# The memory of lines in a Trainium2 kernel: weighing one tile later, the state's decay on ScalarE, the tails added in two operations

## The reference, cut to what matters

```python
write_lines = exterior(w1, w2)            # 6 numbers, scaled to length 1
read_lines = exterior(r1, r2)
Jw = write_lines @ J6
outer = Jw[..., :, None] * Jw[..., None, :]                      # 6 x 6
M_all[t] = sum over s < t of decay ** (t - s) * outer[s]   # written as a scaled cumsum
rd_M = einsum('bhti,bhtij->bhtj', read_lines, M_all)
score_M = sum(rd_M * read_lines); score_M2 = sum(rd_M * rd_M)
alpha = sigmoid(iter_mix)
mem_score = (1 - alpha) * score_M + alpha * score_M2
gated = mean over heads of sigmoid(mem_score * mem_scale) * gate
out = (seq_out + gated * mem_val) @ out_w.T + out_b
```

## Time and profile before

| | us |
|---|---|
| median of 3 runs | 1944.21 (1939.68 to 1946.05) |
| the profiled execution: its time / its span | 1945.89 / 1944.0 |
| PE busy | 1876.9 (97% of the span) |
| DVE busy | 1614.2 (83%) |
| ACT busy | 1501.3 (77%) |
| POOL busy | 916.5 (47%) |
| turns 0 to 5 of the memory of lines, first multiply of turn 0 to the reciprocal | 1149.12 to 1227.41 |
| turns 6 and 7 and the first output chunks | 1227.41 to 1252.40 |

### The profile page before, as it was taken

One profiled execution on the slowest core, in us unless ns is written; L12 is line 12 of the kernel. 1 busy time (PEld: TensorE's weight loads), 2 busy tenths in 40 slices (PEclk: granted clock), 3 DMA queues, 4 the chain that ended last, 5 costly groups with the idle time before them and its releaser, 6 DMA issues. The chain is left out here.

```text
span 1944.0 us, 61233 instructions
## 1 busy us (share of the span) xinstructions
PE 1876.9 (97%) x22590; PEld 1112.2 (57%) x22590; DVE 1614.2 (83%) x5474; ACT 1501.3 (77%) x4121; POOL 916.5 (47%) x548
## 2 busy tenths in 40 slices
PE   7999999999999999999999998899999999999998
PEld 3777763577775343444444367436777635777743
DVE  6899965899995678999999769869999658999855
ACT  5999994799997354777777754469999947999963
POOL 2788860588881040000000046338888506888800
PEclk9999999999999987999999999999999999999999
DMA  6221220122221040111111000002221201222301
GB/s 187 47 50 44 50 62 6 35 46 48 49 62 23 6 160 25 42 41 42 42 42 42 21 6 2 2 19 46 47 50 44 62 6 36 50 48 46 71 12 43
DMA packets 76138, 85.63 MB, mean 44 GB/s; under 512 B 17135, under 2 KB 50499, under 8 KB 75715
## 3 DMA queue, kind: packets, MB, share of 16 engines
q1 hardware_dynamic: 75647, 81.70, 16.8%
q10 hardware_dynamic: 196, 0.02, 0.0%
HBM read 21.16 MB, written 8.39 MB: 15 GB/s over the span
## 5 line engine op out<-in xcount | busy, mean ns | idle before, releaser
L333 ACT ACTIVATE probs<-probs,negmax 128x128 f32<-128x128 f32 x1024 | 401.8, 402 | 1.1 <-DVE negmax L408 0.6
L2170 ACT ACTIVATE gprobs<-ps_global 128x1024 f32<-128x1024 f32 (+3 forms) x384 | 291.5, 811 | 125.7 <-PE ps_global L1635 103.0
L288 POOL TENSOR_TENSOR rot<-rot 128x1024 f32<-128x1024 f32 x128 | 302.6, 2364 | 144.2 <-DVE rot L378 144.2
L294 POOL TENSOR_TENSOR qk<-rot,cnorm 128x1024 f32<-128x1024 f32 x128 | 244.0, 1906 | 170.5 <-issue 146.8
L301 POOL TENSOR_TENSOR probs<-probs,iden 128x1024 f32<-128x1024 f32 x128 | 242.9, 1898 | 45.7 <-DVE iden L416 44.9
L1865 DVE TENSOR_REDUCE maxes<-ps_global 128x1 f32<-128x512 f32 (+2 forms) x384 | 222.1, 639 | 11.4 <-PE ps_global L1598 6.5
L408 DVE CUSTOM_DVE_ANT_0 probs<-ps_attn,masks 128x128 f32<-128x128 f32 x1024 | 226.4, 286 | 0.7 <-issue 0.5
L333 ACT ACTIVATION_READ_ACCUMULATOR probs<-probs,negmax 128x1 f32 x1024 | 204.2, 199 | 0.0
L1593 PE MATMUL ps_global<-kq 48*128 48x512 bf16 (+3 forms) x768 | 197.3, 346 | 7.0 <-DVE maxes L1865 1.8
L374 DVE TENSOR_TENSOR rot<-ps_attn,rotary 128x512 f32<-128x512 f32 x256 | 175.2, 684 | 2.6 <-PE ps_attn L199 2.1
L2100 POOL CAST m_parts<-m_turn 32x128 bf16<-32x128 f32 x16 | 4.5, 281 | 364.4 <-DVE m_turn L1879 364.4
(11 more groups left out here) (220 smaller groups left out, 4531.1 us busy)
## 6 DMA issues: line engine op xcount, KB each, us to landing
v_first<-v_second SPq DMA_DIRECT2D x256, 128.0 KB, 2.3
hs<-z_a SPq DMA_DIRECT2D x256, 32.0 KB, 1.9
ln<-z_b SPq DMA_DIRECT2D x56, 128.0 KB, 2.3
kq<-split_scratch SPq DMA_DIRECT2D x64, 96.0 KB
kq<-split_scratch SPq DMA_DIRECT2D x64, 64.0 KB
split_scratch<-parts SPq DMA_DIRECT2D x8, 384.0 KB, 4.1
split_scratch<-gprobs SPq DMA_DIRECT2D x6, 384.0 KB, 4.1
x_tok<-in_x_dram SPq DMA_DIRECT2D x4, 512.0 KB, 6.4
```

The costliest lines, as they stand in the source:

```text
L288: nc.gpsimd.tensor_tensor(a, a, b, ALU.add).then_inc(C["rot_sum"], 1)
L294: nc.gpsimd.tensor_tensor(qk[:, k % 2, :].rearrange("p (h d) -> p h d", d=DH), rot_a[:, k % 2, :, :], cnorm[:, k % 2, :].unsqueeze(2).to_b ...
L333: last = nc.scalar.activation(probs[:, k % 2, slot, :], probs[:, k % 2, slot, :], ACT.Exp, scale=-1.0, bias=negmax[:, k % 2, slot:slot + 1 ...
L2170: nc.scalar.activation(probs[:, step % RING, 2 * p:2 * p + 2, 0:w], ps[:, S0 + 2 * p:S0 + 2 * p + 2, 0:w], ACT.Exp).then_inc(C["p2_exp"], 1)
```

## The change

Four edits, all in the memory of lines.

1. `weigh(t-1)` instead of `weigh(t)`: in turn t DVE makes blend, weight and score of the tile before, ahead of `sum_squares(t+2, 0)`; in the last turn `weigh(7)` is made as well. The tile `read` becomes double for this.
2. On DVE the last two multiplies (6 and 7) are put ahead of `read_memory(t, 1)`.
3. A new function `fade(t+1)` on ACT, the last of its turns 0 to 5, makes state * decay in four activations of 144 elements into the tile `faded` (a part of `ln_s`). `advance` waits for it and adds the tails from PSUM in two additions of 288 elements; `advance(0)` keeps the four old instructions.
4. ACT's `scale_lines(t)` is moved behind copies 6 and 7.

```diff
-        read, plain, blend = [behind.take(HB * LINE).rearrange("p (x c) -> p x c", x=HB) for _ in range(3)]
+        read = behind.take(2 * HB * LINE).rearrange("p (k x c) -> p k x c", k=2, x=HB)
+        plain, blend = [behind.take(HB * LINE).rearrange("p (x c) -> p x c", x=HB) for _ in range(2)]
...
             def advance(k):
                 wait(dve, "ml_tail", k + 1)
                 wait(dve, "ml_state", k)
...
                 wait(dve, f"ml_row{(k + 1) % 2}", 16 * GROUP * ((k + 1) // 2))
+                if k > 0:
+                    wait(dve, "ml_faded", k)
+                    for half in range(2):
+                        at = slice(half * GROUPS // 2, (half + 1) * GROUPS // 2)
+                        last = nc.vector.tensor_tensor(state[:, (k + 1) % 2, at, :].rearrange("p q n -> p (q n)"),
+                                                       faded[:, at, :].rearrange("p q n -> p (q n)"),
+                                                       ps[:, TAIL_BANKS[half], 0:2 * STATE_ROWS], ALU.add)
+                    last.then_inc(C["ml_state"], 1)
+                    return
...
                 all_terms(5, 6)
+                if valid(t - 1):
+                    weigh(t - 1)
                 if valid(t + 2):
                     sum_squares(t + 2, 0)
+                multiplies(6, 8)
                 if valid(t):
                     read_memory(t, 1)
-                multiplies(6, 8)
-                if valid(t):
+                if t == LAST:
                     weigh(t)
                 if valid(t + 2):
                     clip(t + 2, 0)
...
+            def fade(k):
+                wait(act, "ml_state", k)
+                for q in range(GROUPS):
+                    last = nc.scalar.activation(faded[:, q, :], state[:, k % 2, q, :], ACT.Identity, scale=A["whole"][:, q:q + 1])
+                last.then_inc(C["ml_faded"], 1)
...
-                lefts(2, 5)
-                if valid(t):
-                    scale_lines(t)
-                lefts(5, 6)
+                lefts(2, 6)
                 if valid(t + 2):
                     square_line(t + 2, 0)
                 lefts(6, 8)
+                if valid(t):
+                    scale_lines(t)
                 if valid(t + 2):
                     inverse(t + 2, 0)
                     square_line(t + 2, 1)
                     inverse(t + 2, 1)
+                if 0 < t + 1 < LAST:
+                    fade(t + 1)
```

More of the change, by code:

```diff
@@ L1441, in global_attention_pass @@
             "ml_outer", "ml_tail", "ml_state", "ml_row0", "ml_row1", "ml_m", "ml_term", "ml_read", "ml_plain", "ml_blend", "ml_weight",
-            "ml_score", "ml_turned", "ml_out"))
+            "ml_score", "ml_turned", "ml_out", "ml_faded"))
     U2 = P2_STEPS
@@ L1481, in global_attention_pass @@
         state = shared.take(2 * GROUPS * STATE_ROWS).rearrange("p (k q n) -> p k q n", k=2, q=GROUPS)
+        faded = squares[:, :, :].rearrange("p k t -> p (k t)")[:, 0:GROUPS * STATE_ROWS].rearrange("p (q n) -> p q n", q=GROUPS)
         first = Arena(early[:, :])
@@ L1912, in read_memory @@
                 wait(dve, "ml_term", USES_M * k + (3 if half == 0 else USES_M))
-                nc.vector.reduce_sum(read[:, first * B:end * B, :].rearrange("p x c -> p (x c)"),
+                nc.vector.reduce_sum(read[:, k % 2, first * B:end * B, :].rearrange("p x c -> p (x c)"),
                                      term[:, first * B * PAIRS_6:end * B * PAIRS_6].rearrange("p (x j) -> p x j", j=LINE), AX_X
@@ L1919, in weigh @@
                 wait(dve, "ml_plain", k + 1)
-                flat = read[:, :, :].rearrange("p x c -> p (x c)")
+                flat = read[:, k % 2, :, :].rearrange("p x c -> p (x c)")
                 nc.vector.scalar_tensor_tensor(out=blend[:, :, :].rearrange("p x c -> p (x c)"), in0=flat, scalar=A["alpha"][:, 0:1],
```

## The result

The changed kernel took 1961.74 us (median of 4 runs, 1957.0 to 1963.1) against 1945.13 us before (4 runs, 1939.68 to 1947.17): a ratio of 1.0082, 95% interval 1.007 to 1.0094. It is slower by 16.6 us; 10.8 were forecast, and the range ended at 1961. The profiled execution had a span of 1960.0 us against 1944.0. One later run of the kernel before, in the session of experiments 5 to 8, took 7420.19 us and is left out of every ratio.

What follows compares the result with a forecast made beforehand. DVE was taken to set the turn's period (busy 12.14 of 12.83 us). Per turn -1.67 + 0.56 + 2.15 = +1.04; six turns +6.3 plus last two turns +4.5 gave +10.8, 1955.0 us, range 1949 to 1961.

Steps and rivals of the forecast that it cites:

- a: DVE's stop of 0.55 us before the first sum_squares goes when weigh(t-1) fills it: 0.63 us a turn less.
- b: DVE's weight, moved away from POOL's subtraction, falls from 1.24 to 0.56 us: 0.68 less a turn.
- (c): DVE's advance: two additions at 0.74 us replace four instructions at 1.10, 0.36 less a turn.
- (d): New DVE stop before the second sum_squares, behind multiply 7, POOL's subtraction and ACT's square: 0.56 us a turn lost.
- (e): DVE's advance waits for the fade, last in ACT's turn behind Ln and Exp: 2.15 us a turn lost.
- The six turns: Turns 0 to 5 grow by about 1.04 us each (turn 0 by 1.06): +6.3 us, kept at 4 to 9.
- The last two turns: Turns 6 and 7: late weigh makes PE's turn(5) and turn(6) wait; +4.5 us, bounds 1.7 to 6.
- the fade waits and PE's clock falls too: Rival: idle PE before turn(5) and turn(6) drops its clock, about 1.5 us each time; 1958 us, chance 0.13.
- The tail is hidden: Rival: later chunks leave DVE idle, so the extra weigh costs nothing; +6.3 us, 1950.5 us, chance 0.14.
- The fade is hidden: Rival: advance finds its input ready, period 11.72 us; with the tail 1942 us, no difference; chance 0.08.
- DVE's work alone counts: Rival: every new wait finds its partner early, six turns gain 10.0 us; 1934 us, chance 0.07.

Runs made afterwards that it cites:

- experiments 5 to 8: The session that ran kernel 5, kernel 6, kernel 7 and kernel 8 beside the kernel before, whose median there was 1944.88 us.
- kernel 3: The kernel before with only the fade, last in ACT's turn, and the two additions added: 1961.82 us, ratio 1.0082.
- kernel 1: The changed kernel with only fade(t+1) moved to the start of ACT's turn, behind copy_scores: 1946.35 us, ratio to before 1.0003.
- kernel 2: The changed kernel without the fade and with the old advance of four instructions: 1948.91 us, ratio to before 1.0014.
- kernel 8: kernel 1 with multiplies 6 and 7 put back behind read_memory(t, 1): 1952.15 us, ratio to before 1.0038.
- kernel 5: The changed kernel with weigh(5) also made in turn 5, and turns 6 and 7 making their own weigh: 1955.49 us, ratio to before 1.0052.
- kernel 4: The changed kernel with extra matmuls that nothing reads, put where PE stood idle: 1957.04 us, ratio to before 1.0057.
- kernel 7: kernel 6 plus two unread matmuls of 512 columns on PE behind gate(0) in turn 6: 1940.43 us, ratio to before 0.9977.
- kernel 6: The changed kernel with both repairs, the fade move of kernel 1 and the weigh(5) catch-up of kernel 5: 1940.92 us, ratio to before 0.9984.

## Why the prediction fell short

The direction, the terms of a turn and the waits came out as forecast. The size did not, since the sum had no term for TensorE's clock.

**The stops that go (a, b).** Right. The 0.55 before the first `sum_squares` is gone; the weight takes 0.56 in all eight places. Kernel 3, with `weigh` in its old place, has it at 1.24 again: the Trainium skill's rule (SBUF — State Buffer, "Who interferes with whom"), that an instruction with two SBUF inputs contends with a GpSimd instruction that reads SBUF, agrees with both.

**The additions (c).** 0.73 from the addition to the clip against 0.74 forecast. Right; kernels 1 and 2 show that only 0.12 of the saving counts once the fade is out of the way.

**The new stop (d).** 0.46 of idle time; 0.56 was worked out from start to start, which holds some 0.1 of overlap. Right, and kernel 8 shows that it grows when the multiplies come later.

**The wait for the fade (e).** 2.12 us of idle time where 2.15 were forecast; the turn was 13.90 against 13.87. Kernels 1 and 3 show that this wait comes from the place of the fade on ACT: it goes when only that is moved, and it comes when only the fade is added. The six turns without the clock came to +6.46 against +6.3.

**The last two turns.** The mechanism was right: `turn(5)` and `turn(6)` of PE waited 2.26 us each for the late score, and kernel 5 takes 8.3 us away there by making the score on time (and pays 1.3 of them in turn 5). The size forecast was about half of what came: +4.5 against +8.51. With the clock at 1.00 (kernel 4) the stretch is 27.35 us, 3.16 above before, or 4.4 above the 22.95 that the repaired kernel 7 takes with the clock at 1.00. So the 4.5 was a fair price of the waits alone.

**The step that failed** is the cost of TensorE's clock, which the sum put at nothing. It stood only as the rival "the fade waits and PE's clock falls too", with a chance of 0.13, at about 1.5 us for each of two drops, and was set aside with the reason that "2.2 is shorter than 2.96". The one idle stretch seen ahead of a drop in this stage was taken as if it were the shortest that can lead to one. In the changed kernel one drop followed 1.97 us of idle PE ahead of turn 2, and two came at the end of waits of 2.26 us. The forecast also looked only at the waits before the two transposes, and not at those that the longer turn itself opened on PE: 1.7 to 2.0 us ahead of each of turns 1 to 5 instead of 0.6 to 0.9, and 4.09 instead of 2.96 behind `gate(0)`. The clock cost 1.33 us in turn 2 and 5.35 in the last two turns, where the rival had 3.0 in all. The kernel before had about 1 of this already (the drop in the earlier trace rows). Waits of 9.6 us and a slow clock of 1.33 + 5.35 make the stage's 16.3. Kernel 4 shows it from the other side: it has more work on PE and is 4.7 us faster. The range left no room for it either. With the upper bounds of both terms (9 and 6) the sum reaches 1959.2, and the rival's two drops on top would already have made 1962.2, outside a range that ends at 1961.

One reading was slightly off, without effect: in turns 2 to 5 DVE is busy within 0.02 us of turn 1 (12.12 to 12.16), not 0.01.

**The rivals.** "The tail is hidden" did not happen: the chunks behind took 29.57 us in both kernels. "The fade is hidden" is what kernel 1 made of it: 11.94 a turn, where that rival had 11.72 (the clip then waits for Exp, which I had left out). "DVE's work alone counts" never came about; even with both repairs the stage gains 4.3 us of the 10.0.

**What stays open:** why the clock fell in turn 2 of the changed kernel and not in turns 1, 3, 4 and 5, whose idle stretches of PE are 1.7 to 2.0 us as well. In the fade-alone kernel, where PE stands idle for 2.40 to 2.74 us ahead of turns 1 to 5, it was turns 3 and 5, and not turn 2 with the longest stretch. Before the change 2.13 us of idle PE (1222.75 to 1224.88) passed without a drop, and so did the two waits of 2.26 us in kernel 1; in kernel 7 a drop followed 1.18 us. So the length of one stretch does not tell whether a drop follows, and what does was not tied to anything in these traces. That idle time on PE has to do with it is what kernel 4 shows, where all four drops of the stage went at once. The fastest of the four runs of the changed kernel (1957.0) has a mean clock of 0.984, the others 0.980 or 0.981; that it had fewer drops is likely, but only the one at 1961.85 has a trace.

## What to carry to other kernels

When a step is moved to an engine with time to spare, ask behind what it stands in that engine's order. Four activations, 1.3 us together, cost DVE no stop at the start of ACT's turn and one of 2.1 us a turn at its end, though their input had been ready all along. Shifting a piece of a pipeline one tile later empties the first turn and fills the last, and there is often nothing to hide it there; catch it up in the last full turn, in a wait. And where a change makes PE wait for about 2 us, price the clock too, and let the range hold it: a matmul list with pauses may run at half speed for the next few microseconds, in one turn and not in the next.

## What the hardware showed unexpectedly

- After idle stretches of PE of 1.97 us (turn 2) and of 2.26 us (turns 6 and 7) windows at a granted clock of 0.50 follow, and one drop begins inside the stretch of 4.09 us; before the change the only drop of this stage followed 2.96 us. The shortest stretch seen right ahead of a drop is 1.18 us (kernels 7 and 8), and stretches of up to 2.74 us (kernel 3) passed without one. Matmuls that nobody reads, put into the stretches, kept it at 1.00 and made the program 4.7 us faster.
- A scalar_tensor_tensor with two SBUF inputs is held up by POOL as the tensor_tensor is: in turn 7 of the changed kernel the blend took 1.32 us beside POOL's product of the sigmoids (L2170, 1.26 us), against 0.61 elsewhere. Kernels 1, 2, 4 and 8 show the same 1.32 for the last blend; in kernels 3, 5, 6 and 7, where no blend falls beside that product, none is above 0.62.

```profile
1258.90 1.32 DVE L1923 SCALAR_TENSOR_TENSOR gprobs<-gprobs,alpha 128x384 f32<-128x384 f32 x1
```
